# An audio tower on one core: three of eight heads read as whole tables instead of two, and gathers of eight tokens of one head

## The reference

```
q      = x @ Wq_pk                        # two halves of 32 features for each of 8 heads
sim    = q . pk_keys                      # 64 keys per half
scores, idx = top_k(sim, 16)              # 16 best keys of each half
score  = scores[0][:, None] + scores[1][None, :]     # 256 pairs
final_scores, pk_idx = top_k(score, 16)   # 16 best pairs: rows of a table of 64*64 = 4096
w      = softmax(final_scores)
k      = sum over the 16 rows of w * keys_table[row + 4096 * head]
v      = the same with values_table
out    = causal softmax attention of (x @ Wq) with k and v over 375 tokens, then @ Wo
```

## Time and profile before

| | |
|---|---|
| median of 3 runs | 9001.16 us (8988.16 to 9004.75) |
| the profiled execution | 8921.69 us, its span 8919.9 us |
| mean granted clock of TensorE, as a share of full speed | 0.66 |
| busy time: PE, DVE, ACT, POOL | 5811.1, 3250.8, 2088.5, 4374.7 us |
| gathers (POOL L429) | 4512, 966 ns each |

### The profile page before, as it was taken

The page is one execution under the profiler, slowest core; times in us unless marked ns, Lnnn a source line. Parts: engine busy times, 40 slices in busy tenths (PEclk is TensorE's granted clock), DMA queues, the critical chain, the costliest instruction groups (busy, mean ns, idle before and its releaser), DMA issues.

```text
span 8919.9 us, 86784 instructions
## 1 busy us (share of the span) xinstructions
PE 5811.1 (65%) x23616; PEld 3849.5 (43%) x23616; DVE 3250.8 (36%) x14095; ACT 2088.5 (23%) x4517; POOL 4374.7 (49%) x4574
## 2 busy tenths in 40 slices
PE   1367576575766757676665767667576666757677
PEld 1244444353444534444443544445344443534443
DVE  4334242433423243342424334232433423243036
ACT  0112122121322213132221312222131222222143
POOL 3454545545454554545455454545545445554500
PEclk9567566666756667675666667566666756666577
DMA  1111111111111111111111111111111111111100
GB/s 41 51 41 32 39 34 37 44 31 39 30 40 35 39 41 32 41 31 41 35 38 42 32 40 32 39 35 40 40 31 39 33 36 38 39 36 32 41 12 14
DMA packets 166480, 321.90 MB, mean 36 GB/s; under 512 B 82044, under 2 KB 90836, under 8 KB 165774
## 3 DMA queue, kind: packets, MB, share of 16 engines
q0 software_dynamic: 144384, 295.20, 12.5%
q1 hardware_dynamic: 21230, 20.00, 0.8%
q10 hardware_dynamic: 288, 0.07, 0.0%
HBM read 310.37 MB, written 4.61 MB: 35 GB/s over the span
## 4 chain that ended last, share of the span: by engine, by line
PE 36%; another core or an unknown queue 25%; issue 20%; DVE 14%; ACT 5%; DVEq 0%; ACTq 0%; DMA 0%; SPq 0%
PE gath L615 7%; PE accu L477 5%; PE dense L469 4%; PE work L668 2%; PE dense L464 2%; PE sims L662 2%; ACT past L902 2%; PE dense L470 1%; PE work L643 1%; PE work L698 1%; PE work L544 1%; PE work L655 1%; DVE front L1244 1%; DVE i L1243 1%
## 5 line engine op out<-in xcount | busy, mean ns | idle before, releaser
L429 POOL DMA_INDIRECT store<-in,idx_now x4512 | 4358.2, 966 | 3970.7 <-PE gath L615 2195.0
L615 PEld LDWEIGHTS gath<-wbd,store 128*128 128x128 f32 (+1 forms) x9024 | 1607.2, 266 | 783.7 <-issue 747.5
L615 PE MATMUL gath<-wbd,store 128*128 128x8 f32 (+1 forms) x9024 | 1553.7, 304 | 551.5 <-issue 432.8
L469 PE MATMUL dense<-parts_f,hot 128*128 128x375 bf16 x3072 | 905.0, 416 | 495.3 <-issue 420.7
L477 PE MATMUL accu<-dense_w,store 128*128 128x375 f32 x2048 | 1123.8, 640 | 11.9 <-issue 10.1
L902 ACT ACTIVATE past<-dense,edge 128x375 bf16<-128x375 f32 x1024 | 587.0, 573 | 2176.3 <-remote 1338.9
L464 PE MATMUL dense<-ranksT,hot 128*128 128x375 bf16 x1008 | 407.8, 405 | 847.1 <-ACT past L902 678.7
L469 PEld LDWEIGHTS dense<-parts_f,hot 128*128 128x128 bf16 x3072 | 322.2, 114 | 894.0 <-issue 820.6
L910 ACT ACTIVATE dense_w<-dense 128x375 f32<-128x375 f32 x1024 | 493.8, 482 | 887.3 <-remote 547.3
L464 PEld LDWEIGHTS dense<-ranksT,hot 128*128 128x128 bf16 x1008 | 158.4, 157 | 1083.0 <-issue 1033.7
L477 PEld LDWEIGHTS accu<-dense_w,store 128*128 128x128 f32 x2048 | 500.1, 258 | 142.2 <-issue 107.6
(11 more groups left out here) (285 smaller groups left out, 6983.9 us busy)
## 6 DMA issues: line engine op xcount, KB each, us to landing
store<-in,idx_now POOLq DMA_INDIRECT x4512
x_in<-in SPq DMA_DIRECT2D x16, 187.5 KB
store<-in SPq DMA_DIRECT2D x1, 2048.0 KB, 8.7
queries_kept<-n3T SPq DMA_DIRECT2D x16, 93.8 KB
h_saved<-h SPq DMA_DIRECT2D x16, 93.8 KB
store<-queries_kept SPq DMA_DIRECT2D x16, 93.8 KB, 2.4
store<-h_saved SPq DMA_DIRECT2D x16, 93.8 KB
out<-store SPq DMA_DIRECT2D x16, 93.8 KB
```

What stands on the lines that cost most here:

```text
L429: nc.gpsimd.indirect_dma_start(rows[0:slots, r * PER + i, :], None, kv_table, bass.IndirectOffsetOnAxis(ap=idx_now[0:slots, at:at + 1], ax ...
L469: mm(dense[:, 1, 0:S], hot[:, c, :], parts[:, k, h, :], start=(k == 0), stop=False)
L615: last = mm(gath[:, 0, at:at + 8], rows[0:slots, r * PER + i, :], wbd[0:slots, t * GATHERS + n, :], start=True, stop=True)
```

## The change

A third head becomes dense, five stay gathered. A gather now holds eight tokens of one head (128 rows, always full), so a tile has 80 gathers in ten groups. DVE spreads weights and row numbers over eight columns each with a mask (`eights`), and `turn_picks` gathers them with ten matmuls of 16 columns. DVE writes the turned row numbers straight to `idx_now`, after a wait for `freed`; POOL's copy goes. The ring has six groups. The ranks and pair scores of the third dense head use the bank of `accu`, so the copies between PE, ACT and DVE there come in two parts. The third dense head brings two more search pieces to the picks of each tile. The tables of the fills are others; so are the copies that move finished halves out of `gath` (two simple ones), and `shared` and `picks` lend space for new tiles.

```diff
--- before.py
+++ after.py
-HD = 2
+HD = 3
 HG = H - HD
 HH = 2
-QUADS = P // 4
-GATHERS = 3 * QUADS + 1
+EIGHT = 8
+BLOCK = SLOTS // EIGHT
+GATHERS = HG * BLOCK
 PER = 8
-GROUPS = -(-GATHERS // PER)
+GROUPS = GATHERS // PER
...
-RING = 9
+RING = 6
...
-PICK_STEPS = 15 + 2 * (HG // HH + 2 * HD)
+PARTS = [(a, min(a + HH, HG)) for a in range(0, HG, HH)]
+PICK_STEPS = 15 + 2 * (len(PARTS) + 2 * HD)
 FAR = 1024.0
-FILL_TURN = ((0, 0), (0, 0))
-FILL_PREPARE = ((2, 2), (1, 2), (2, 1), (1, 2), (2, 1), (1, 2), (2, 1), (1, 1), (2, 0))
-FILL_GRADIENT = ((3, 1), (0, 1), (0, 0), (0, 1), (2, 1))
-FILL_FIRST = ((5, 2), (3, 2))
-FILL_SECOND = ((11, 6), (7, 4))
-GROUPS_INSIDE = (0, 0, 1, 1, 1, 1, 1, 1)
+FILL_TURN = ((0, 2), (0, 1))
+FILL_PREPARE = ((2, 1), (2, 1), (3, 1), (2, 1), (3, 1), (2, 0), (3, 0), (2, 0), (3, 0))
+FILL_GRADIENT = ((3, 1), (2, 0), (2, 0), (2, 1), (3, 1))
+FILL_FIRST = ((8, 3), (4, 2))
+FILL_SECOND = ((15, 5), (10, 4))
+GROUPS_INSIDE = (0, 1, 1, 1, 1, 1, 0, 0)
...
-FIRST_HEAD, STEPS_A, STEPS_B = 2, (1, 1, 1, 1, 1, 1, 0, 0), (2, 2, 2, 2, 2, 2, 0, 0)
+FIRST_HEAD, STEPS_A, STEPS_B = 2, (1, 1, 1, 1, 1, 1, 0, 0), (3, 3, 3, 3, 3, 3, 0, 0)
...
+        eights = sb("eights", [P, EIGHT + BLOCK])
...
+        w_wide = picks[0:P, 0:HG * SLOTS].rearrange("p (h m k) -> p h m k", h=HG, k=K)
+        i_wide = picks[0:P, HG * SLOTS:2 * HG * SLOTS].rearrange("p (h m k) -> p h m k", h=HG, k=K)
...
-        idx_next = sb("idx_next", [128, NT * GATHERS], U32)
...
+        three_banks = (dense[:, 0], dense[:, 1], accu[:, 0])
...
                     pool.wait_ge(s["next_ready"], b * NT + t + 1)
-
-                    nc.gpsimd.tensor_copy(idx_now[:, gathers(t)], idx_next[:, gathers(t)]).then_inc(s["idx_taken"], 1)
-                    pool.wait_ge(s["idx_taken"], b * NT + t + 1)
                     for g in range(GROUPS):
...
-                for c, src in enumerate((wgt[:, 0:HG].rearrange("p h k -> p (h k)"), idxf[:].rearrange("p h k -> p (h k)"))):
-                    tr(work[0:HG * K, c, 0:P], src, ident[0:P, 0:P])
-                    for m in range(3):
-                        last = mm(work[HG * K:SLOTS, c, tile(m)], src[:, m * 32:(m + 1) * 32], ident[0:P, 0:P], start=True, stop=True)
+                for c, src in enumerate((w_wide, i_wide)):
+                    for h in range(HG):
+                        last = mm(work[:, c, h * BLOCK:(h + 1) * BLOCK], src[:, h].rearrange("p m k -> p (m k)"), eights[:, EIGHT:], start=True, stop=True)
                 last.then_inc(s["tw_mm"], 1)
...
             def keep_ranks(b):
                 act.wait_ge(s["rank_mm"], b + 1)
-                nc.scalar.copy(ranksT[:], dense[:, :, 0:S]).then_inc(s["rank_done"], 1)
+                nc.scalar.copy(ranksT[:, 0:2], dense[:, :, 0:S])
+                nc.scalar.copy(ranksT[:, 2], accu[:, 0, 0:S]).then_inc(s["rank_done"], 1)
...
-                v.tensor_tensor(wgt[:], wgt[:], esum[:, 1, :].unsqueeze(2).broadcast_to([P, H, K]),
-                                ALU.mult).then_inc(s["wgt_done"], 1)
+                v.tensor_tensor(i_wide, idxf[:].unsqueeze(2).broadcast_to([P, HG, EIGHT, K]),
+                                eights[:, 0:EIGHT].unsqueeze(1).unsqueeze(3).broadcast_to([P, HG, EIGHT, K]), ALU.mult)
+                v.tensor_tensor(wgt[:, 0:HG], wgt[:, 0:HG], esum[:, 1, 0:HG].unsqueeze(2).broadcast_to([P, HG, K]),
+                                ALU.mult).then_inc(s["w_done"], 1)
+                dve.wait_ge(s["w_done"], n)
+                v.tensor_tensor(w_wide, wgt[:, 0:HG].unsqueeze(2).broadcast_to([P, HG, EIGHT, K]),
+                                eights[:, 0:EIGHT].unsqueeze(1).unsqueeze(3).broadcast_to([P, HG, EIGHT, K]), ALU.mult).then_inc(s["wgt_done"], 1)
                 yield
                 dve.wait_ge(s["tw_mm"], n)
                 if not (isinstance(b, int) and b == 0):
-                    dve.wait_ge(s["idx_taken"], b * NT + (t + 1 - NT))
...
+                    dve.wait_ge(s["freed"], b * (NT * GROUPS) + ((t + 1 - NT) * GROUPS + RING))
+                v.tensor_copy(idx_now[:, gathers(t)], work[:, 1, 0:GATHERS]).then_inc(s["next_ready"], 1)
```

More of the change, by code:

```diff
@@ L40 @@
 STEP = 15
[L41 removed]
+HD = 3
 HG = H - HD
 HH = 2
[L44 to L45 removed]
+EIGHT = 8
+BLOCK = SLOTS // EIGHT
+GATHERS = HG * BLOCK
 PER = 8
[L47 to L48 removed]
+GROUPS = GATHERS // PER
+SIZES = [PER] * GROUPS
 HALF_GROUPS = GROUPS // 2
 HALF_AT = PER * HALF_GROUPS
[L51 removed]
+assert GATHERS == 2 * HALF_AT and HALF_AT * 2 == HG * BLOCK and HALF_AT % BLOCK == BLOCK // 2
+RING = 6
 RING_LAPS = NT * GROUPS // RING
[L53 removed]
+assert NT * GROUPS == RING * RING_LAPS
 CHUNKS = NKV // 128
@@ L485, in turn_ranks @@
                     for t in range(NT):
-                        last = tr(dense[:, h, tile(t)], ranks[:, t, h, :], ident[0:P, 0:P])
+                        last = tr(three_banks[h][:, tile(t)], ranks[:, t, h, :], ident[0:P, 0:P])
                 last.then_inc(s["rank_mm"], 1)
@@ L493, in pair_scores @@
                 for h in range(HD):
-                    mm(dense[:, h, 0:S], pair_w[:, h, :], n2T[:], start=True, stop=True, skip_group_check=True)
+                    mm(three_banks[h][:, 0:S], pair_w[:, h, :], n2T[:], start=True, stop=True, skip_group_check=True)
                     for t in range(NT):
-                        last = mm(dense[SUB:128, h, tile(t)], zneg[:, t, h:h + 1].broadcast_to([P, SUB]), ident[0:P, 0:P],
+                        last = mm(three_banks[h][SUB:128, tile(t)], zneg[:, t, h:h + 1].broadcast_to([P, SUB]), ident[0:P, 0:P],
                                   start=False, stop=(t == NT - 1), skip_group_check=True)
@@ L612, in take_group @@
                     n = g * PER + i
-                    slots = SLOTS if n < GATHERS - 1 else HG * K
-                    at = (n - half * HALF_AT) * 8
-                    last = mm(gath[:, 0, at:at + 8], rows[0:slots, r * PER + i, :], wbd[0:slots, t * GATHERS + n, :],
+                    at = (n - half * HALF_AT) * EIGHT
+                    last = mm(gath[:, 0, at:at + EIGHT], rows[:, r * PER + i, :], wbd[:, t * GATHERS + n, :],
                               start=True, stop=True)
@@ new lines, in keep_half @@
+                at = 0 if half == 0 else SLOTS // 2
+                src = gath[:, 0, at:at + HG // 2 * SLOTS].rearrange("p (h n) -> p h n", n=SLOTS)
+                nc.scalar.copy(kvT[:, whole, tile(t)], src[:, :, 0:P])
+                if half == 0:
+                    nc.scalar.copy(kvT[:, HG // 2, t * P:t * P + SLOTS // 2],
+                                   gath[:, 0, HG // 2 * SLOTS:HG // 2 * SLOTS + SLOTS // 2]).then_inc(s["kv_done"], 1)
+                else:
+                    nc.scalar.copy(kvT[:, HG // 2, t * P + SLOTS // 2:(t + 1) * P],
+                                   gath[:, 0, 0:P - SLOTS // 2]).then_inc(s["kv_done"], 1)
@@ L1310, in pick_rows @@
                 yield
-                for c in range(HG // HH):
-                    at = slice(c * HH, (c + 1) * HH)
-                    v.tensor_tensor(pick, places[:, at].unsqueeze(3).broadcast_to([P, HH, K, CAND]),
-                                    cidx[:, at].unsqueeze(2).broadcast_to([P, HH, K, CAND]),
+                for c, (first, end) in enumerate(PARTS):
+                    at, n_at = slice(first, end), end - first
+                    some = pick[:, 0:n_at]
+                    v.tensor_tensor(some, places[:, at].unsqueeze(3).broadcast_to([P, n_at, K, CAND]),
+                                    cidx[:, at].unsqueeze(2).broadcast_to([P, n_at, K, CAND]),
                                     ALU.bitwise_xor).then_inc(s["pick_step"], 1)
                     at_step(16 + 2 * c)
-                    v.tensor_reduce(idxf[:, at], pick, AX_X, ALU.min).then_inc(s["pick_step"], 1)
+                    v.tensor_reduce(idxf[:, at], some, AX_X, ALU.min).then_inc(s["pick_step"], 1)
                     at_step(17 + 2 * c)
```

64 lines of the change are left out of this document (23 added, 41 removed).

## The result

The changed kernel takes 9383.40 us (median of 4 runs, 9375.28 to 9409.58) against 8994.66 us before: a ratio of 1.0428, 95% interval 1.0386 to 1.0471. It is slower by 4.3% where the forecast was 2.4%, and inside the range. The profiled execution of the kernel before (8921.69 us) is 73 us shorter than this median, so a difference from its trace is some 4 to 5 us a pass too large; by the medians the change costs 24 us for each of the 16 batches, where the forecast was 13.5.

What follows compares the result with a forecast made beforehand. Bound: PE's work outside attention plus what POOL's gather bursts take from it. Terms 57.5 - 16.5 + 3.5 + 1 - 7 - 25 = +13.5 us a pass, +216 over 16 batches: 9220 us, range 8680 to 9540.

Steps and rivals of the forecast that it cites:

- F: Slow stretches outside attention: shorter gather bursts cut prepare's from 49 to 24 us, -25 us a pass; second fill unchanged.
- the rule: Outside attention, engines slow down from 13 us of unbroken gather issuing by POOL until it pauses; mechanism unknown.
- The 109 us: Loss per pass: ten slow stretches total 132 us, in which PE does 23 us of work.
- A: 32 added dense steps a pass, 6 in attention at 1.44 us and 26 outside at 1.88: +57.5 us.
- the clock rival: Longer matmul runs lift PE's clock outside attention: -17.5 us a pass, 8719 us; sign: prepare's clock above 0.75; chance 0.14.
- C: The turn: PE waits for DVE's search, weights and products, partly covered by two groups at the ranksT wait: +3.5 us.
- D: Turned picks: ten products of 16 columns replace eight turnings per tile, +1 us for three tiles.
- B: Fewer gather groups on PE, 36 to 30 a pass at 2.75 us each: -16.5 us.
- E: Gradient: dense steps fill PE's 7.1 us wait at L729, -7 us a pass.
- At nothing: Booked as costless: row numbers written by DVE, ring of six, POOL's 42 fewer gathers, one more table loaded in the prologue.

Runs made afterwards that it cites:

- e2: Changed kernel with a POOL pause of six small writes after each group of eight gathers: 8146.49 us, ratio 0.9054 to the kernel before.
- e7: Changed kernel with the six-write pause, six dense steps moved from attention to prepare, and two more calls of the picks: 8028.19 us, ratio 0.8904.
- e3: Kernel before with a POOL pause of six small writes after each group: 7864.96 us, ratio 0.8732.
- e11: Kernel before with a POOL pause of four small writes after each group: 7412.79 us, ratio 0.8287.
- e5: Kernel before with a POOL pause of two small writes after each group: 9064.17 us, ratio 1.0058.
- e6: Kernel before with the six-write POOL pause after every second group only: 8867.92 us, ratio 0.9840.
- e4: Changed kernel with six dense steps moved from attention to prepare: 9196.74 us, ratio 1.0211 to the kernel before.
- e8: Kernel before with DVE writing row numbers straight to the gathers' buffer, without POOL's copy: 9004.08 us, ratio 0.9997.
- e9: Changed kernel with two dense heads and the ring and tables of before, keeping gathers of eight tokens (96 a tile): 9060.89 us, ratio 1.0149.

## Why the prediction was right, and where it was not

**The direction** came from the right balance: dense steps cost more than fewer groups and shorter slow stretches give back. e2 and e7 against e3 show the same order with most of the slow time gone. **The size** is partly luck: misses of 35 us a pass in one direction and 17 in the other (last line of this section) leave the 18 that kept the time inside the range.

**F, slow stretches: right in place, size and cause, wrong in the rule.** By the rule, prepare's 49 us were to become 24; over all passes the rule's time there went from 50.8 to 26.9 (the slow time from 35 to 15), and in the second fill it stayed (49.4 and 52.9). e2, e3 and e11 show the cause, gathers that POOL issues too closely. The rule "slow from 13 us of unbroken issuing until POOL pauses" fails in e5 and e6. The 109 us that I took as lost in a pass are neither shown nor refuted: e11 gained 95 with all else kept, while POOL became the bound.

**A, dense steps: the term that was mis-sized.** "In attention I take 1.44: 6 x 1.44 = 8.6": measured 3.1 each, 18.4 (e4). I priced it by one step in an undisturbed place, at the full clock, though attention's clock was 0.83 (0.78 over all passes). But the mean clock of a stage doesn't explain the price: outside I chose 1.88, and the six steps moved to prepare cost 1.4 each, with a clock that rose from 0.73 to 0.77. In attention, at 0.75, the 2.4 us of busy time for a step lie nearer to the half clock's 2.77 than to 1.44; why the added steps run so slowly there stays open. In prepare the clock rival was half right: its 0.73 stayed just below the 0.75 that I had set for it. What the other steps outside cost wasn't separated. The rest of attention's growth, 9 us (125.6 in e4 against 116.5), isn't settled; 6 of them are longer waits of PE, two more searches of DVE lie there, and it isn't the place of the steps.

**C, the turn: right in its main step, too low in the rest.** DVE's order in the changed kernel, at the end of attention:

```profile
3623.65 1.22 DVE L1325 TENSOR_REDUCE ranks<-picks 125x64 f32<-125x1024 uint32 x1
3629.02 0.35 DVE L1395 TENSOR_TENSOR h<-h_now,work 125x192 f32<-125x192 f32 x1 [4.15 <-PE work L706]
3629.53 1.22 DVE L1321 TENSOR_TENSOR picks<-places_s,keys 125x1024 uint32<-125x1024 uint32 x1
...
3632.37 0.28 DVE L1330 TENSOR_REDUCE esum<-wgt 125x8 f32<-125x128 f32 x1 [0.26 <-DVE ranks L1325]
...
3634.42 0.82 DVE L1341 TENSOR_TENSOR picks<-wgt,eights 125x640 f32<-125x640 f32 x1
```

and PE's, where turn_picks waits 7.43 us:

```profile
3627.91 0.86 PE L706 MATMUL work<-ident,two_q 64*125 64x64 f32 x3 [0.73 <-ACT two_q L1041]
3636.20 4.42 PE L601 MATMUL work<-eights,picks 125*128 125x16 f32 x20 [7.43 <-DVE picks L1341]
```

From the addition's end (3629.37) DVE needs until 3635.24 for search, weights and both products: 5.9 us where I had 5.65. The waits of PE in that pass, as in the earlier trace rows:

```profile
PE dense L467 <- ACT past L903: 56.5, 17, 15.1
PE dense L472 <- issue: 37.1, 13, 9.3
PE dense L472 <- ACT dense_w L911: 23.5, 10, 7.1
...
PE work L601 <- DVE picks L1341: 7.4, 1, 7.4
PE work L730 <- DVE halves L1429: 5.4, 1, 5.4
```

The wait at `ranksT` is gone, as forecast. But it was worth less than I charged: the 8.0 us of the earlier trace rows are nearly the longest of 14 passes, whose mean is 4.1 (2.4 to 8.1). The turn grew by 10.7 us with 8.25 us of groups in it, and the products with `eights` took 0.9 us longer than the turnings, so C and D are 9.7 us instead of 4.5. The first three rows are PE behind ACT and issue at the dense steps, in slow stretches and elsewhere.

**B and D: right in size.** Groups cost 1222.2 us for 480, 2.55 us each against 2.75. D was +1 for three tiles; the third tile's products alone took 0.9 more.

**E, the gradient: wrong.** The wait at L729 was to be gone, -7. It is still there in the changed kernel, at L730 (the last row above): 5.45 us in the mean of all passes against 7.13, so -1.7. Two dense steps stand ahead of it in place of a group. That gradient and its neighbours moved by 0.8 us, near the 3.4 forecast, came from other terms there, which no run separates.

**At nothing: right for the row numbers,** by the time of e8. That the packing of eight tokens is neutral, which the sum assumed, isn't borne out: e9 is 6.5 us a pass longer, with six gathers more.

Summed: attention 22 us too low, the turn 5 and the first fill 8 too low, prepare 10, the second fill 4 and the gradient's part 3 too high. What made the first fill longer isn't known.

## What to carry to other kernels

When several engines that wait for different things slow down together, look for an engine that issues indirect DMAs in long unbroken runs, and let it rest: here 2.09 us after each eight gathers gave 17%, where the rebalancing of dense and gathered heads cost 4.3%. Don't price an added step by its best timeline, nor by a stage's mean clock: move a few steps between stages and measure (e4: 3.1 and 1.4 us). Read a wait that a sum rests on in more than one pass. And try a part alone (e8, e9) where the sum books it at nothing.

## What the hardware showed unexpectedly

After eight gathers (10 us), 1.28 us of rest on POOL leaves 94 us of slow time a pass, 2.09 us leaves 13; after sixteen, 2.91 us leaves 88. A mean rate between eight gathers in 11.3 us and eight in 11.8 us would tell these kernels apart as well. During the slow stretches DVE is slowed with PE, though it issues no DMA. In the kernel before, in the slow stretch from 3775 on, its short instructions start 0.7 or 1.4 us apart, idle before them with no releaser named:

```profile
3788.22 0.18 DVE L1265 TENSOR_TENSOR cidx<-i16f 125x24 uint32<-125x24 f32 x1 [1.21 <-issue]
3788.91 0.18 DVE L1265 TENSOR_TENSOR cidx<-i16f 125x16 uint32<-125x16 f32 x1 [0.51 <-issue]
3790.31 0.18 DVE L1265 TENSOR_TENSOR cidx<-i16f 125x16 uint32<-125x16 f32 x1 [1.22 <-issue]
```

ACT starts little there too, but the profile has it wait for others, so whether it is slowed itself isn't shown.

The gathers themselves don't queue up: by the trace's packets a gather's data has landed 2.2 us (median) after its issue in the kernel before, and 2.1 us with four writes. The Trainium skill (Runtime: NRT & Kernel Launch, Instruction fetch mechanics) says that sequencers stream their instructions through DMA queues of their own and that this is mostly hidden. Slowed fetching would fit engines that stop for nothing visible; against it, from 3514 to 3530 in the kernel before the trace has packets of the gathers' queue alone, none of the two instruction queues that it shows elsewhere. Those two need not be all, so the mechanism stays open. Every execution timed here has a recorded span and clock, so no run shows whether the stretches are there when nothing is recorded.
